# Copying the turned queries on ScalarE instead of VectorE, and turning them before the keys, in one attention of a fused two-block model

## The reference, cut to what matters

```
qkv = x @ Wqkv.T + bqkv                        # x: layer norm of the residual stream
q, k, v = split(qkv), 16 heads of 8 columns each
q = q / sqrt(mean(q*q) + 1e-6) * wq ;  k likewise with wk     # per head
attn = softmax(q . k over 256 keys)            # no mask, no 1/sqrt(d)
z = attn . v ;  out = z @ Wo.T + bo ;  x = x + out
```

## Time and profile before

| | us |
|---|---|
| median of 3 runs (2067.97 to 2069.43) | 2068.7 |
| the profiled execution's own time | 2076.66 |
| its span, first to last instruction | 2074.8 |
| a2's rows of work, of that span | about 1505 to 1870 |
| TensorE busy in the span | 1720.9 (83%) |
| VectorE busy | 1351.2 (65%) |
| ScalarE busy | 1224.9 (59%) |
| GpSimd busy | 1112.0 (54%) |

### The profile page before, as it was taken

One profiled execution on the slowest core, in us unless ns is written; L12 is line 12 of the kernel. 1 busy time (PEld: TensorE's weight loads), 2 busy tenths in 40 slices (PEclk: granted clock), 3 DMA queues, 4 the chain that ended last, 5 costly groups with the idle time before them and its releaser, 6 DMA issues. The chain is left out here.

```text
span 2074.8 us, 46088 instructions
## 1 busy us (share of the span) xinstructions
PE 1720.9 (83%) x14912; PEld 1194.3 (58%) x14912; DVE 1351.2 (65%) x4112; ACT 1224.9 (59%) x2906; POOL 1112.0 (54%) x1932
## 2 busy tenths in 40 slices
PE   4989999978787887879699988799868888879984
PEld 2668888866443333444355555699723444338974
DVE  3468888845663555457587886365568778756554
ACT  2346666653553776746266655578635666567863
POOL 3136566643364555436567658545367565543574
PEclk9989999999897999989699999899958899899998
DMA  6664000000002000000000000145300000013544
GB/s 145 104 182 108 1 1 1 1 1 0 1 1 52 1 2 2 1 1 1 1 2 2 2 3 30 53 124 140 82 7 18 9 9 4 15 41 85 134 114 124
DMA packets 110963, 83.25 MB, mean 40 GB/s; under 512 B 16698, under 2 KB 101803, under 8 KB 110604
## 3 DMA queue, kind: packets, MB, share of 16 engines
q1 hardware_dynamic: 102316, 63.05, 12.4%
q0 software_dynamic: 8416, 17.29, 2.7%
HBM read 51.78 MB, written 31.12 MB: 40 GB/s over the span
## 5 line engine op out<-in xcount | busy, mean ns | idle before, releaser
L2149 ACT ACTIVATE a2prob<-PS 128x512 f32<-128x512 f32 x256 | 144.0, 598 | 96.8 <-PE PS L1879 96.8
L1629 DVE TENSOR_REDUCE a2mx<-PS 128x4 f32<-128x1024 f32 x128 | 155.7, 1219 | 35.5 <-PE PS L1855 34.4
L2149 ACT ACTIVATE a1prob<-PS 128x384 f32<-128x384 f32 x256 | 116.4, 491 | 75.1 <-PE PS L1879 74.1
L2152 ACT ACTIVATE a0prob<-PS 128x1024 f32<-128x1024 f32 x128 | 127.3, 1027 | 51.9 <-PE PS L1879 51.5
L1629 DVE TENSOR_REDUCE a1mx<-PS 128x6 f32<-128x768 f32 x128 | 122.0, 953 | 48.9 <-PE PS L1862 47.1
L1450 POOL TENSOR_SCALAR_AFFINE_SELECT a1prob<-a1prob 128x256 f32<-128x256 f32 x256 | 97.9, 411 | 67.8 <-ACT a1prob L2149 66.7
L2855 PE MATMUL PS<-k_W2e,m1bhid 128*128 x624 | 85.8, 281 | 13.0 <-DVE m1byo L2743 12.8
L83 PE MATMUL PS<-identb,parts 128*128 128x128 bf16 x1024 | 81.6, 229 | 15.2 <-DVE parts L1644 8.2
L2699 POOL DMA_INDIRECT gy<-rows_out,pos x64 | 61.0, 953 | 60.0 <-DMA rows_out<-m1byo 16.2
L2844 PE MATMUL PS<-m1bxT,m1bw 128*128 128x128 f32 x624 | 88.2, 286 | 5.8 <-ACT m1bxT L2887 4.0
L2844 PE MATMUL PS<-m1axT,m1aw 128*128 128x128 f32 x624 | 86.9, 283 | 5.0 <-ACT m1axT L2887 3.9
(11 more groups left out here) (536 smaller groups left out, 5325.4 us busy)
## 6 DMA issues: line engine op xcount, KB each, us to landing
cv_im<-turned SPq DMA_DIRECT2D x48, 129.0 KB, 4.5
m1awr<-expert_rows SPq DMA_DIRECT2D x77, 66.0 KB
m1bwr<-expert_rows SPq DMA_DIRECT2D x77, 66.0 KB
rows_in<-la_blank SPq DMA_DIRECT2D x78, 64.0 KB, 1.6
rows_out<-m1ayo SPq DMA_DIRECT2D x38, 128.0 KB
m1axin<-rows_in SPq DMA_DIRECT2D x35, 128.0 KB
rows_marked<-in_blank_rows SPq DMA_DIRECT2D x39, 65.0 KB, 2.3
m1bxin<-rows_marked SPq DMA_DIRECT2D x19, 130.0 KB
```

What stands on the lines that cost most here:

```text
L1629: v.tensor_reduce(mx[:, 2 * j:2 * j + 2, :], bank[:, :, 0:SEG * seg_len].rearrange("p h (s n) -> p h s n", n=seg_len), AX.X, ALU.max).then ...
L2149: act.activation(prob[:, h % RING, 0:n_prob], SB[(b * NH + h) % NSB][:, 0:n_prob], ACT.Exp, scale=scale).then_inc(s["exp"], 1)
L2152: act.activation(prob[:, h % RING:h % RING + EXPS, :], PS[:, h % NSB:h % NSB + EXPS, :], ACT.Exp, scale=scale).then_inc(s["exp"], EXPS)
```

## The change

In a2 alone (`if weights`), and in the steps alone: VectorE no longer has `take_q`, ScalarE gets it ahead of `take_k`, and TensorE turns the queries first and then the keys. Rows 0 and 1, ahead of the steps, stay as they were. ScalarE's new function waits for the same two semaphores that VectorE's waited for in this attention.

```diff
 # VectorE, step(b)
-                        if h == AT["qT"]:
+                        if h == AT["qT"] and not weights:
                             take_q(b + AHEAD2)
...
 # TensorE, step_with_max(b), h == AT["turns"]
+                        if weights:
+                            turn_q(b + AHEAD2)
                         turn_k(b + AHEAD2)
-                        turn_q(b + AHEAD2)
+                        if not weights:
+                            turn_q(b + AHEAD2)
...
 # ScalarE
+            def take_q(b):
+                finished(act, s["top"], (b - 1) * PAIRS - 1)
+                act.wait_ge(s["qt"], b + 1)
+                act.activation(qT[:, b % 2].rearrange("p g n -> p (g n)"), bank_q.bitcast(BF16), ACT.Copy)\
+                   .then_inc(s["qT"], 1)
...
 # ScalarE, step(b)
                     if h == AT["kT"] and b + AHEAD2 < B:
+                        if weights:
+                            take_q(b + AHEAD2)
                         take_k(b + AHEAD2)
```

## The result

The changed kernel takes 2075.65 us in the median of 19 runs, the kernel before 2067.97 us in 19 runs beside it: ratio 1.0039 [1.0024, 1.0055], that is 8.1 us slower [5.0, 11.4]. The forecast was 4.5 us slower.

What follows compares the result with a forecast made beforehand. A ring of TensorE's matmuls and VectorE's maximum bounds most; gapless ScalarE sets the pace in steps 3, 5, 7, 9. 3.55 + 0.8 - 1.2 - 0.25 = 2.9 us queues, plus 1.6 clock: 4.5 slower, 2073.2 us (2067.0 to 2078.5).

Steps and rivals of the forecast that it cites:

- Four router steps, 3.55 us: Steps 3, 5, 7, 9: ScalarE's added copies delay the second scaling and TensorE's router turns, 3.55 us lost in all.
- Scores of heads 12 and 13 held: Steps 2, 12, 13: scores wait for head 10's later exponential, 0.2 us in step 2, 0.3 each otherwise, 0.8 lost.
- Steps 10 and 11, 0.60 gained each: There VectorE's router choice delays maximum 5; without the copy it starts 0.60 us sooner, 1.2 us gained in all.
- Nothing gained by VectorE elsewhere: Outside steps 10 and 11, the maximum without the copy waits for its matmuls, gaining 0.0 to 0.1 us.
- R2: Rival: relieving VectorE starts pair 5's maximum sooner in all 14 steps, 8.4 us gained, 2060.3 us; chance 0.08.
- R3: Rival: ScalarE's delays stay hidden and TensorE keeps the earlier queries, 2.8 us gained, 2065.9 us; chance 0.10.
- R1: Rival: queue delays only, no new fall of TensorE's clock, 2.9 us slower, 2071.6 us; chance 0.28.
- R4: Rival: each of the 14 copies holds TensorE by its full 0.92 us, 12.9 us slower, 2081.6 us; chance 0.08.
- the clock in steps 5 and 9: Sign: TensorE's granted clock there tells the forecast, with a new fall, from the queues-only rival, with none.
- Queries first at nothing: Queries ready 0.2 us sooner in most steps, counted as no gain in the router steps and steps 2, 12, 13.
- the five steps of step 8's kind: Steps where scores already started after the delayed exponential: no loss, and 0.05 us gained each from queries first, 0.25 in all.
- The clock, 1.6 us: Longer TensorE idle before router turns may halve the clock in steps 5 and 9; one fall of two, 1.6 us.

Runs made afterwards that it cites:

- e3: The whole change plus six matmuls with unread results before the router's turns in steps 3, 5, 7 and 9, against the kernel before: 2073.27 us, 1.0041.
- a1: The changed kernel run a second time, unedited, against the kernel before: 2075.38 us, 1.0031.
- e1: The change made only in the four router steps 3, 5, 7 and 9, against the kernel before: 2077.61 us, 1.0057.
- e7: The whole change, but in steps 3, 5, 7 and 9 VectorE copies the keys, against the kernel before: 2071.45 us, 1.0009.
- e4: Only the order changed, queries turned first, their copy left on VectorE, against the kernel before: 2071.72 us, 1.0042.
- e5: The change made only in steps 10 and 11, against the kernel before: 2065.59 us, 0.9994.
- e2: The change made only in the ten steps without the router, against the kernel before: 2071.82 us, 1.0024.
- e9: Second sample of the change made only in the ten steps without the router, against the kernel before: 2071.88 us, 1.0016.
- e6: The change in steps 10 and 11 alone, plus three unused matmuls before the router's turns, against the kernel before: 2063.64 us, 0.9985.
- e8: Second sample of the change in steps 10 and 11 plus three unused matmuls before the router's turns, against the kernel before: 2065.10 us, 0.9989.
- e10: The change made only in steps 2, 12 and 13, against the kernel before: 2068.99 us, 1.0008.

## Why the prediction was right, and where it was mis-sized

- *Four router steps, 3.55 us: shown.* 7.14 us without a gap for 6.22, idle of 1.41 to 1.45 us before the turns, step 9 longer by 0.99 (0.96 in e3, 0.99 in a1), where 0.92 was forecast. In step 5 ScalarE's run grew by 0.77 (6.37 to 7.14) for the 0.79 forecast; the gap there is 0.03 us in the sums of the earlier trace rows, not 0.13. e1 has the loss with these steps alone, e7 takes step 9's away by taking away ScalarE's second copy, and e4 has half of it there.
- *Scores of heads 12 and 13 held, 0.3 each in steps 12 and 13: shown for step 13, not for step 12.* Step 13 before and in the changed kernel, at full clock:

```profile
1810.33:1828.12 17.79, 14.87 (x179) 7.32 (x179) 13.83 (x22) 11.87 (x23) 13.28 (x17) 1.00 0.10 34
```

```profile
1805.61:1823.74 18.13, 14.92 (x179) 7.32 (x179) 13.34 (x21) 12.57 (x23) 13.49 (x17) 1.00 0.11 35
```

  It is 0.34 longer. In step 12 the scores wait 0.25 us for an exponential, which the earlier trace rows did not, but the step is only 0.04 longer than in e5, which leaves it as before (first e5, then the changed kernel; the last row is these scores):

```profile
1772.75:1792.06 19.31, 16.70 (x185) 8.21 (x185) 14.63 (x27) 12.67 (x25) 14.42 (x21) 1.00 0.09 28
```

```profile
1786.26:1805.61 19.35, 16.71 (x185) 8.21 (x185) 14.12 (x26) 13.26 (x27) 14.41 (x21) 1.00 0.09 28
...
1801.39 0.39 PE L1879 MATMUL PS<-a2qM,a2kT 32*128 32x256 bf16 x4 [0.25 <-ACT a2prob L2158]
```

- *Steps 10 and 11, 0.60 gained each: shown in step 10* (25.13 to 24.53 us in e5, 24.53 in the changed kernel); in step 11 maximum 5 starts 1.45 us after maximum 4's end, before 2.05.
- *Nothing gained by VectorE elsewhere: shown* for the steps named above. R2 has fallen, and R3 with it; R1 (2.9 us) and R4 (12.9) lie outside the measured 8.1 [5.0, 11.4]. R1 is outside by its time only: by the sign that was to tell it from the forecast, the clock in steps 5 and 9, the first trace is R1's. The Trainium skill ("Perfetto Trace Analysis", Identifying the Most-Contended Engine) would have the engine of highest occupancy worked on first. Over the whole stretch, with TensorE set aside, that is VectorE, and handing its copies to ScalarE cost 1.0039 [1.0024, 1.0055]: ScalarE, with the lower occupancy, was the full one in four stretches.
- *Queries first at nothing: mis-sized in e4*, where the order alone costs 0.47 us in step 9. In the whole change this is no extra term, since the new copy takes the place of `take_k`. The 0.25 us left for the five steps of step 8's kind are not seen: steps 4, 6 and 8 take 17.23 to 17.24 us at full clock in the changed kernel, and 17.24 to 17.25 in e5, which leaves them as before.
- *The clock, 1.6 us: the step that failed.* The prediction put it at one new fall behind the router's turns in steps 5 or 9. In the changed kernel's first trace both kept full clock, after idles of 1.41 us, and steps 3 and 7 fell to half clock, as before. In its second trace (a1) step 5 fell, as forecast, but step 3 did not:

```profile
1619.41 0.63 PE L83 MATMUL PS<-k_ident,m1bn 128*128 128x128 f32 x4 [1.44 <-ACT m1bn L2358]
...
1662.73 1.09 PE L83 MATMUL PS<-k_ident,m1bn 128*128 128x128 f32 x4 [1.40 <-issue]
```

  So two of the four steps fall behind the turns in both traces of before and in both of the change: the falls there are no more than before. Yet over all executions the mean clock is 0.0031 ± 0.0021 lower, 3.7 us by the line of time on clock. e3 shows that filling those idles does not bring it back, e2 with e9 that ten steps without any router's turns lose as much (0.0033). The traces point to steps 13 and 14: 34.2 us in both of before, 36.1 and 37.3 in the changed kernel's two, 39.7 and 42.6 in e2's and e9's. But e1, e5, e6 and e8, which leave those steps as before, also took 36.6 to 37.9 there in their one trace each, and e10 did not settle it.

So the direction came from the queue terms, and the size was short by 3.6 us [0.5, 6.9]. The forecast's 4.5 us lies just below the measured interval, and it came that near with a clock term whose place was wrong: that part is luck. By the estimate about 2.1 of the shortfall is in the clock (3.7 for 1.6) and 2.6 ± 1.1 at equal clock (5.5 for 2.9), together more than there is to explain, since the means of all executions differ by 9.2 us and the first sample by 8.1.

The traces do not bear the 2.6 us out. Four times step 9's 0.99, with 0.34 and 0.04 for steps 13 and 12 and twice 0.60 off for steps 10 and 11, is 3.1 us of queues, an estimate from steps that could be compared, near the forecast's 2.9. A likelier reading, argued and not tested, is that the one slope prices the clock of these steps too low. In e1 step 13, which e1 leaves as it was, takes 21.47 us at a clock of 0.76, for 17.79 at 1.00:

```profile
1822.06:1843.53 21.47, 18.17 (x179) 8.53 (x179) 13.93 (x22) 11.95 (x22) 16.04 (x20) 0.76 0.12 38
```

That is 3.7 us for 0.24 of 21.47, which is 0.0025 of the whole span: 1.5 us for each 0.001. At that price the clock lost by the change (0.0031) costs 4.6 us and leaves 4.6 of the 9.2 for the queues. What stays open is in which steps the mean clock falls and by what, and whether the queues cost more than the 3.1 us that could be compared.

## What to carry to other kernels

Judge an engine by the stretch in which the work is put, not by its share of the span: a copy that takes 1.02 us on an engine that is 63% busy cost its full 0.92 us in the four stretches without a gap, 0.34 us in step 13, and in the queues of the other steps next to nothing. Before work is taken off the busiest engine, see what its next instruction waits for: if that is another engine's work started only when the one before ends, the time comes back as idle. And where TensorE's clock varies from one execution to the next, price a shift by many executions and their mean clock, since one profile can show the slower kernel as the faster one.

## What was not expected of the hardware

- The kernel before took 2058 to 2078 us over its 128 executions, at mean granted clocks of 0.912 to 0.929, correlation -0.80 (-0.86 over the executions of all kernels, where 1.19 us go with each 0.001). About two thirds of the variance between executions of one program goes with TensorE's mean clock.
- An idle of 1.41 us before the turns was followed by full clock in steps 5 and 9, one of 1.45 us by half clock in step 3 (0.63 and 1.09 us for the same four matmuls). In a second execution of the same kernel 1.44 us in step 3 was followed by full clock and 1.40 us in step 5 by half clock. The length of that idle alone does not decide.
